# Two local-attention stacks: the unshifted half of the feed forward's input read in place, statistics in two halves, weight loads taken off the shifting steps

## Chip, core and metric

The kernel runs on one core of one Trainium2 chip. The metric is the device time of one execution in microseconds. The median over several executions is compared. Engine names are those of the profile: PE is TensorE (matmuls and transposes), PEld its weight loads, DVE is VectorE, ACT is ScalarE, POOL is GpSimd, and SPq is the queue of the sync engine, which here issues every DMA.

## What is computed

A chain of layers over x of shape (2, 1024, 128), fp32. Two identical stacks of six layers (`local_stack`, tags `l_` and `m_`) take two thirds of the time, and only they are changed. One layer of a stack:

```python
def shift_tokens(t):
    a, s = jnp.split(t, 2, -1)
    s = jnp.pad(s, ((0, 0), (1, 0), (0, 0)))[:, :-1]
    return jnp.concatenate([a, s], -1)
...
def ffn_layer(x, g, bln, W1, b1, W2, b2):
    mu = x.mean(-1, keepdims=True)
    var = ((x - mu) ** 2).mean(-1, keepdims=True)
    xn = (x - mu) / jnp.sqrt(var + 1e-05) * g + bln
    hg = xn @ W1 + b1
    a, gate = jnp.split(hg, 2, -1)
    return a * jax.nn.gelu(gate, approximate=False) @ W2 + b2
for i in range(DEPTH):
    x = attn_layer(shift_tokens(x), Wqkv[i], q_scale[i], k_scale[i], Wo[i]) + x
    x = ffn_layer(shift_tokens(x), ln_g[i], ln_b[i], W1[i], b1[i], W2[i], b2[i]) + x
```

So the feed forward sees each token's own first 64 features and the last 64 of the token before it. `attn_layer` is windowed attention (window 32, 16 heads of 64) with rotary tables.

## The kernel before

**Tiles.** 128 tokens lie on the 128 partitions; a stack has 16 tiles, in 4 groups of 4. `Y` (which is the buffer `XN`) holds the stream, tile by tile. Over six layers there are NL = 96 tiles and FG = 24 groups per stack.

**Steps.** Each engine's program is written out by hand as one loop over steps s. In step s the engines work on several tiles at once: PE projects q and k of tile s+2, takes scores of tile s, v of tile s, and finishes tile s-1 (turn of the weights, `values`, `output_turn`, `output`). `phase(s, k)` gives group g in step 4g+k. A group g of the feed forward goes through: step 4g+4 `shift` (SPq), 4g+5 `statistics` (DVE) and `root` (POOL), 4g+6 `middle` (DVE), `normalise` and `gelu` (ACT), `norm_turn4` and `up` (PE), 4g+7 `down`, 4g+8 the turn for the next layer. Every engine runs its instructions strictly in that written order, with semaphores between engines.

**The shift.** In `shift(g)` the queue waits for `y_add` (DVE has added the attention output of the group's last tile) and then issues copies within the on-chip memory into `xsh`: L1694 the unshifted half of all 128 partitions, L1695 the shifted half of 127 partitions, L1697 partition 127's rows to partition 0, and for even groups L1700, one more row. `statistics(g)` (L1508 to L1516) and `normalise(g)` (L1387) read `xsh`.

**What the queue does besides.** `spread_v(s)` (L1685, L1686, L1688, ten copies a step) waits for `V_out` (ACT's copy of v, L1363) and spreads v into the windows that `values(s)` (PE, L1221) reads one step later. The next layer's weights are loaded by pairs of DMAs (L1655, L1658) in the steps i = 2 to 8 of the 16 of a layer, after the shift where i is 4 or 8, and the feed forward's weights in i = 9.

**ACT around `normalise`.** In a step 4g+6 ACT runs: squares of q, `normalise`, squares of k (L1346), exponents (L1334), `values_out` (L1352, the copy of PE's result O to SBUF), copy of v. PE's `output_turn` (transposes at L1152 with `O` in their name, "the O turn" below) waits for both copies of `values_out`.

**DVE and POOL around it.** After `statistics`, POOL's `root` (L1615) takes the power of the variances, then POOL runs the roots of the next tile (L1574 to L1580) and scales its k (L1586). DVE's `middle` (L1521) is 128x4 elements, and ACT's `normalise` waits for it.

Of the kernel before, what the change touches and what calls it, by code (L numbers as in the profile page):

```python
# [53 lines left out]
def build(nc, t, out):  # L54
    ctx = ExitStack()
    with ctx:
        te, ve, ac, gp, sp = nc.tensor, nc.vector, nc.scalar, nc.gpsimd, nc.sync
        every = []

        def signals(names):  # L60
            made = [ctx.enter_context(nc.semaphore(n)) for n in names.split()]
            every.extend(made)
            return made

        def sb(name, *shape):
            return ctx.enter_context(nc.sbuf_tensor(name, list(shape), F32))
# [3 lines left out]
        V, G = Chain(ve, dve_own), Chain(gp, pool_own)  # L70
# [10 lines left out]
        xn4 = sb("xn4", P, 2, 4, D)  # L81
# [817 lines left out]
        def linear_attention():  # L899
# [170 lines left out]
        rq_out, rk_out, ssr_out, ss_out, rn_out, ms_out, rsum_out, y_add = signals(  # L1070
            "l_rq_out l_rk_out l_ssr_out l_ss_out l_rn_out l_sub_out l_rsum_out l_y_add")
# [4 lines left out]
        v_spread, w_attn, w_rot, w_ffn, shifted = signals("l_v_spread l_w_attn l_w_rot l_w_ffn l_shifted")  # L1076
# [3 lines left out]
        def local_stack(tag):  # L1080
            with ExitStack() as own:
                def sl(name, *shape, dtype=F32):
                    return own.enter_context(nc.sbuf_tensor(tag + name, list(shape), dtype))
                Y = XN
# [22 lines left out]
                mx = sl("mx", P, 2, 8)  # L1107
                sm, rs = sl("sm", P, 2 * 8), sl("rs", P, 2 * 8)
                O, oT = sl("O", P, 8, 2, LD), sl("oT", P, 8, P)
                xsh, xnorm = sl("xsh", P, 2, 4, D), xn4[:, 0, :, :]  # L1110
                xnT = xn4[:, 1, :, :].rearrange("p j d -> p (j d)")
                fst, fmv, frs, fmid, fneg = sl("fst", P, 4, 6), sl("fmv", P, 4, 2), sl("frs", P, 4), sl("fmid", P, 4), sl("fneg", P, 4)
                sums2 = sl("sums2", P, 2 * LH, 2)
                zero, eps = sl("zero", P, 4), sl("eps", P, 4)
                gl, hT = xT4, sl("hT", P, 3, 512)
# [16 lines left out]
                def phase(s, k):  # L1132
                    g, r = divmod(s - k, 4)
                    return g if r == 0 and 0 <= g < FG else None
# [187 lines left out]
                def act():  # L1322
# [60 lines left out]
                    def normalise(g):  # L1383
                        ac.wait_ge(fmid_out, g + 1)
                        at_ge(ac, n_turn, g)
                        for j in range(4):
                            m = ac.activation(xnorm[:, j, :], xsh[:, g % 2, j, :], ACT.Identity, scale=frs[:, j:j + 1], bias=fmid[:, j:j + 1])  # L1387
                        m.then_inc(xnorm_out)

                    def copy_norm(g):  # L1390
# [15 lines left out]
                    for s in range(-2, 4 * FG + 8):  # L1406
# [10 lines left out]
                        if widened is not None:  # L1417
                            normalise(widened)
# [26 lines left out]
                def dve():  # L1445
# [55 lines left out]
                        ve.tensor_tensor(Y[:, i, :], PS[:, 5, 0:D], Y[:, i, :], ALU.add).then_inc(y_add)  # L1501

                    def statistics(g):
                        ve.wait_ge(shifted, 64 * (g // 2 + 1) + 48 * ((g + 1) // 2))
                        V.wait()
                        at_ge(ve, xnorm_out, g)
                        for j in range(4):
                            m = ve.bn_stats(fst[:, j, :], xsh[:, g % 2, j, :])  # L1508
                        V.step(m)
                        V.wait()  # L1510
                        for j in range(4):
                            m = ve.bn_aggr(fmv[:, j, :], fst[:, j, :])
                        V.step(m)
                        V.wait()
                        ve.tensor_tensor(fneg[:, :], zero[:, :], fmv[:, :, 0], ALU.subtract)
                        ve.tensor_tensor(frs[:, :], fmv[:, :, 1], eps[:, :], ALU.add).then_inc(fvar_out)  # L1516
# [51 lines left out]
                def pool():  # L1568
# [63 lines left out]
                    for s in range(-2, 4 * FG + 8):  # L1632
# [15 lines left out]
                        if s % NT == 8 and layer(s) + 1 < DEPTH:  # L1648
                            rotary(layer(s) + 1)

                def transfers():
                    def load_attention(l, k):
                        if k < 12:
                            part = slice(k * 256, (k + 1) * 256)
                            sp.dma_start(wqkv[:, l % 2, part], t["l_wqkv"][l][:, part]).then_inc(w_attn, 16)  # L1655
                        else:
                            half = slice((k - 12) * 4, (k - 11) * 4)
                            sp.dma_start(wo[:, l % 2, half, :], t["l_wo"][l].rearrange("(c p) d -> p c d", p=P)[:, half, :]).then_inc(w_attn, 16)  # L1658
# [31 lines left out]
                    def shift(g):  # L1690
                        par, tiles = g % 2, slice(4 * (g % NG), 4 * (g % NG) + 4)
                        sp.wait_ge(y_add, 4 * g + 4)
                        at_ge(sp, xnorm_out, g)
                        sp.dma_start(xsh[:, par, :, 0:D // 2], Y[:, tiles, 0:D // 2]).then_inc(shifted, 16)  # L1694
                        sp.dma_start(xsh[1:P, par, :, D // 2:], Y[0:P - 1, tiles, D // 2:]).then_inc(shifted, 16)  # L1695
                        inner = slice(tiles.start, tiles.stop - 1)
                        sp.dma_start(xsh[0:1, par, 1:, D // 2:], Y[P - 1:P, inner, D // 2:]).then_inc(shifted, 16)  # L1697
                        if par == 0:
                            last = tiles.stop - 1
                            sp.dma_start(xsh[0:1, 1, 0, D // 2:], Y[P - 1:P, last, D // 2:]).then_inc(shifted, 16)  # L1700

                    load_rotary(0)
                    for k in range(14):
# [2 lines left out]
                    for s in range(-2, 4 * FG + 8):  # L1706
                        if 0 <= s < NL:
                            spread_v(s)
                        done = phase(s, 4)
                        if done is not None:  # L1710
                            shift(done)
                        l, i = layer(s) + 1, s % NT
                        if 0 <= s and l < DEPTH:
                            if i == 1:
                                if l >= 2:
                                    sp.wait_ge(rk_out, NT * (l - 1))
                                load_rotary(l)
                            if i == 2:
                                if l >= 2:
                                    sp.wait_ge(v_pr, NT * (l - 1))  # L1720
                                    sp.wait_ge(out_pr, NT * (l - 1))
                            if 2 <= i < 9:
                                load_attention(l, 2 * (i - 2))
                                load_attention(l, 2 * (i - 2) + 1)
                            if i == 9:
                                if l >= 2:
                                    sp.wait_ge(f_down, NG * (l - 1))
                                load_ffn(l)
# [86 lines left out]
```

## Time and profile before

| | |
|---|---|
| median of 3 runs | 4630.66 us (4624.55 to 4635.63) |
| the profiled execution | 4626.41 us, span 4625.1 us |
| PE busy over the span | 3912.4 us, 85% |
| DVE, ACT, POOL busy | 71%, 55%, 54% |
| the two stacks | from about 1030 to 2735 us and 2905 to 4620 us |
| matmuls and weight loads | 67048 each |

The span is the time from the first to the last instruction. Times below are microseconds from the start of the span. A row of the timeline gives the start, the duration, the engine, the line, the tensors and how many instructions are merged in it; in brackets stands how long the engine sat idle just before, and what released it. Where several merged instructions overlap, the duration is from the first start to the last end.

### The profile page before, as it was taken

Reading aid. Unit: us, or ns where it says so; the run is one execution under the profiler, and the core shown is the slowest. Engines: PE = TensorE matmul, PEld = TensorE weight load, DVE = VectorE, ACT = ScalarE, POOL = GpSimd, SP = SyncE. Lnnn points to the kernel's source line nnn. Section 1 sums busy time; section 2 is a strip of 40 time slices with the busy share of each in tenths; the row PEclk is TensorE's granted clock in tenths of the full one; section 3 lists DMA queues with packets and bytes.
Section 4 is the critical chain, followed back from the end, with each engine's and each line's share of the span. In section 5 each row is a group of like instructions: output and inputs, shape, how many; then the busy total and the mean of one; then the engine's idle time right before and its main releaser. Section 6 shows DMA issues by size and latency. Waiting matters only on the chain. (4 is left out here: it accounts for less than half of the span.)

```text
span 4625.1 us, 159303 instructions
## 1 busy us (share of the span) xinstructions
PE 3912.4 (85%) x67048; PEld 2719.8 (59%) x67048; DVE 3275.4 (71%) x6709; ACT 2524.5 (55%) x4765; POOL 2493.8 (54%) x2057
## 2 busy tenths in 40 slices
PE   6868566628999999999999943699999999999996
PEld 3435344415666666666666632466666666666764
DVE  6749526857777777777777726777777777777773
ACT  2323222205676766667667620466666676676664
POOL 2211001117767667676766700676676767667662
PEclk8869787969999999999999965799999999999998
DMA  0010000003333233333222210232333333233222
GB/s 14 1 32 1 10 1 31 5 18 83 82 83 91 67 90 81 82 87 83 78 73 71 71 29 0 74 91 70 86 80 83 87 83 84 67 92 82 70 68 53
DMA packets 307781, 281.44 MB, mean 61 GB/s; under 512 B 158840, under 2 KB 205568, under 8 KB 307072
## 3 DMA queue, kind: packets, MB, share of 16 engines
q1 hardware_dynamic: 307072, 271.25, 23.0%
q8 instruction: 535, 8.77, 0.8%
q14 instruction: 174, 1.43, 0.1%
HBM read 56.14 MB, written 1.05 MB: 12 GB/s over the span
## 5 line engine op out<-in xcount | busy, mean ns | idle before, releaser
L1346 ACT ACTIVATE l_sq<-PS 128x512 f32<-128x512 f32 x384 | 225.8, 595 | 198.4 <-PE PS L1199 161.1
L1346 ACT ACTIVATE m_sq<-PS 128x512 f32<-128x512 f32 x384 | 225.7, 595 | 198.1 <-PE PS L1199 159.3
L124 POOL TENSOR_TENSOR rstd<-rstd,minus_half 128x4 f32<-128x4 f32 x40 | 41.8, 1044 | 518.7 <-DVE rstd L120 518.7
L1611 POOL TENSOR_TENSOR m_Pm<-m_Pm,m_rs 128x1024 f32<-128x1024 f32 x96 | 182.7, 1903 | 236.2 <-DVE m_rs L1483 236.2
L1611 POOL TENSOR_TENSOR l_Pm<-l_Pm,l_rs 128x1024 f32<-128x1024 f32 x96 | 182.8, 1904 | 235.1 <-DVE l_rs L1483 235.1
L1470 DVE TENSOR_TENSOR m_QR<-PS,m_rot 128x512 f32<-128x512 f32 x192 | 131.8, 687 | 164.8 <-ACT m_sq L1346 164.7
L1470 DVE TENSOR_TENSOR l_QR<-PS,l_rot 128x512 f32<-128x512 f32 x192 | 131.8, 687 | 163.5 <-ACT l_sq L1346 163.5
L1501 DVE TENSOR_TENSOR XN<-PS,XN 128x128 f32<-128x128 f32 x192 | 56.2, 292 | 265.0 <-PE PS L1251 264.9
L1606 POOL TENSOR_TENSOR m_QR<-m_QR,m_UQ 128x1024 f32<-128x1024 f32 x96 | 227.8, 2373 | 24.0 <-DVE m_UQ L1473 24.0
L1606 POOL TENSOR_TENSOR l_QR<-l_QR,l_UQ 128x1024 f32<-128x1024 f32 x96 | 227.7, 2372 | 23.8 <-DVE l_UQ L1473 23.8
L1606 POOL TENSOR_TENSOR m_KR<-m_KR,m_UK 128x1024 f32<-128x1024 f32 x96 | 226.8, 2362 | 0.2 <-DVE m_UK L1473 0.2
L1606 POOL TENSOR_TENSOR l_KR<-l_KR,l_UK 128x1024 f32<-128x1024 f32 x96 | 226.8, 2362 | 0.2 <-DVE l_UK L1473 0.2
L1488 DVE TENSOR_REDUCE l_sums<-l_sq 128x16 f32<-128x1024 f32 x192 | 219.1, 1183 | 0.0
L1488 DVE TENSOR_REDUCE m_sums<-m_sq 128x16 f32<-128x1024 f32 x192 | 219.1, 1183 | 0.0
L1221 PEld LDWEIGHTS PS<-m_V,m_pT 64*32 64x32 f32 x12288 | 132.6, 106 | 120.5 <-issue 66.3
L1221 PEld LDWEIGHTS PS<-l_V,l_pT 64*32 64x32 f32 x12288 | 131.5, 106 | 117.8 <-issue 73.0
L1205 PE MATMUL PS<-m_wqkv,XNT 128*128 128x512 f32 x384 | 194.1, 628 | 0.0
L1205 PE MATMUL PS<-l_wqkv,XNT 128*128 128x512 f32 x384 | 192.5, 624 | 0.0
L1199 PE MATMUL PS<-m_wqkv,XNT 128*128 128x512 f32 x384 | 190.9, 620 | 0.6 <-DVE m_UK L1473 0.6
L1199 PE MATMUL PS<-l_wqkv,XNT 128*128 128x512 f32 x384 | 190.4, 618 | 0.5 <-DVE l_UK L1473 0.5
L1221 PE MATMUL PS<-m_V,m_pT 64*32 64x64 f32 x12288 | 155.1, 228 | 41.6 <-DMA m_V<-m_Vt 27.7
L1251 PE MATMUL PS<-l_wo,l_oT 128*128 128x128 f32 x1536 | 189.1, 277 | 0.7 <-ACT l_oT L1358 0.7
(387 smaller groups left out, 11907.7 us busy)
## 6 DMA issues: line engine op xcount, KB each, us to landing
l_V<-l_Vt SPq DMA_DIRECT2D x576, 128.0 KB
m_V<-m_Vt SPq DMA_DIRECT2D x576, 128.0 KB
l_V<-l_Vt SPq DMA_DIRECT2D x384, 64.0 KB
m_V<-m_Vt SPq DMA_DIRECT2D x384, 64.0 KB
l_wqkv<-l_wqkv_dram SPq DMA_DIRECT2D x72, 128.0 KB, 2.4
m_wqkv<-l_wqkv_dram SPq DMA_DIRECT2D x72, 128.0 KB, 2.4
l_rot<-l_rot_dram SPq DMA_DIRECT2D x24, 256.0 KB, 3.6
m_rot<-l_rot_dram SPq DMA_DIRECT2D x24, 256.0 KB, 3.6
```

The source lines that it names most:

```text
L124: gp.tensor_tensor(rstd[:, g % 2, :], rstd[:, g % 2, :], minus_half[:, 0:4], ALU.pow).then_inc(rstd_out)
L1199: te.matmul(PS[:, 2 + b, :], tile_T(n), weights(n, INNER + b * 512, INNER + (b + 1) * 512), start=True, stop=True).then_inc(k_pr)
L1205: m = te.matmul(PS[:, r, :], tile_T(n), wv, start=True, stop=True)
L1221: m = te.matmul(PS[LW * w:LW * (w + 1), 6 + r, c * LD:(c + 1) * LD], pT[64 * r:64 * r + 64, c, LW * w:LW * (w + 1)], V2[64 * r:64 * r + 64 ...
L1251: m = te.matmul(PS[:, 5, 0:D], oT[:, c, :], wo[:, layer(n) % 2, c, :], start=(c == 0), stop=(c == 7))
L1346: ac.activation(sq[:, c, b * 512:(b + 1) * 512], PS[:, 2 * c + b, :], ACT.Square).then_inc(sq_out)
L1470: ve.tensor_tensor(R[:, n % 2, heads, :], src, over(rot[:, par, 2 * c, i, :], 1, [P, 8, LD]), ALU.mult)
L1488: ve.tensor_reduce(sums2[:, c * LH:(c + 1) * LH, 0], sq[:, c, :].rearrange("p (h d) -> p h d", d=LD), AX, ALU.add).then_inc(ssr_out)
L1501: ve.tensor_tensor(Y[:, i, :], PS[:, 5, 0:D], Y[:, i, :], ALU.add).then_inc(y_add)
L1606: gp.tensor_tensor(R[:, n % 2, :, :], R[:, n % 2, :, :], U[:, :, :], ALU.add).then_inc((aq_out, ak_out)[c])
L1611: gp.tensor_tensor(pm, pm, over(rs[:, :], 2, [P, 16, 2 * LW]), ALU.mult).then_inc(pn_out)
```

## The change

Three edits, in both stacks.

- `xsh` holds only the shifted half (64 features). The copy L1694 is gone, one DMA less per group, 48 in all. `normalise` makes each tile in two ACTIVATEs of 64 columns, one from `Y` and one from `xsh`: eight instead of four per group.
- `statistics` takes `bn_stats` of the first half from `Y` before it waits for the shift, and of the second half from `xsh` behind that wait: eight instructions of 64 columns instead of four of 128. `bn_aggr` joins both.
- The pairs of weight loads go to the steps i = 2, 3, 5, 6, 7, 9, 10 of a layer (`LOADS`), and the feed forward's weights to i = 11, so that no step with a shift (i = 0, 4, 8, 12) issues one.

```diff
-                xsh, xnorm = sl("xsh", P, 2, 4, D), xn4[:, 0, :, :]
+                xsh, xnorm = sl("xsh", P, 2, 4, D // 2), xn4[:, 0, :, :]
...
                         ac.wait_ge(fmid_out, g + 1)
                         at_ge(ac, n_turn, g)
                         for j in range(4):
-                            m = ac.activation(xnorm[:, j, :], xsh[:, g % 2, j, :], ACT.Identity, scale=frs[:, j:j + 1], bias=fmid[:, j:j + 1])
+                            for lo, half in ((0, Y[:, 4 * (g % NG) + j, 0:D // 2]), (D // 2, xsh[:, g % 2, j, :])):
+                                m = ac.activation(xnorm[:, j, lo:lo + D // 2], half, ACT.Identity, scale=frs[:, j:j + 1], bias=fmid[:, j:j + 1])
                         m.then_inc(xnorm_out)
...
                     def statistics(g):
-                        ve.wait_ge(shifted, 64 * (g // 2 + 1) + 48 * ((g + 1) // 2))
-                        V.wait()
+                        ve.wait_ge(y_add, 4 * g + 4)
                         at_ge(ve, xnorm_out, g)
                         for j in range(4):
-                            m = ve.bn_stats(fst[:, j, :], xsh[:, g % 2, j, :])
+                            ve.bn_stats(fst[:, j, 0, :], Y[:, 4 * (g % NG) + j, 0:D // 2])
+                        ve.wait_ge(shifted, 48 * (g // 2 + 1) + 32 * ((g + 1) // 2))
+                        V.wait()
+                        for j in range(4):
+                            m = ve.bn_stats(fst[:, j, 1, :], xsh[:, g % 2, j, :])
                         V.step(m)
...
+                LOADS = (2, 3, 5, 6, 7, 9, 10)
...
-                        sp.dma_start(xsh[:, par, :, 0:D // 2], Y[:, tiles, 0:D // 2]).then_inc(shifted, 16)
-                        sp.dma_start(xsh[1:P, par, :, D // 2:], Y[0:P - 1, tiles, D // 2:]).then_inc(shifted, 16)
+                        sp.dma_start(xsh[1:P, par, :, :], Y[0:P - 1, tiles, D // 2:]).then_inc(shifted, 16)
                         inner = slice(tiles.start, tiles.stop - 1)
-                        sp.dma_start(xsh[0:1, par, 1:, D // 2:], Y[P - 1:P, inner, D // 2:]).then_inc(shifted, 16)
+                        sp.dma_start(xsh[0:1, par, 1:, :], Y[P - 1:P, inner, D // 2:]).then_inc(shifted, 16)
...
-                            if 2 <= i < 9:
-                                load_attention(l, 2 * (i - 2))
-                                load_attention(l, 2 * (i - 2) + 1)
-                            if i == 9:
+                            if i in LOADS:
+                                load_attention(l, 2 * LOADS.index(i))
+                                load_attention(l, 2 * LOADS.index(i) + 1)
+                            if i == 11:
```

The queue SPq of stack `l_`, at the first shift: the copies of v (`l_V<-l_Vt`) of one step, the shift (`l_xsh<-XN`), a load of the next layer's weights, and the copies of v of the next step begin. Before:

```order
L1688 DMA l_V<-l_Vt 64x512 x3
L1694 DMA l_xsh<-XN 128x4x64
L1695 DMA l_xsh<-XN 127x4x64
L1697 DMA l_xsh<-XN 1x3x64
L1700 DMA l_xsh<-XN 1x16x4
L1655 DMA l_wqkv<-l_wqkv_dram 128x256 x2
L1685 DMA l_V<-l_Vt 32x512
```

The same place in the changed kernel (its lines are numbered 5 or 6 higher here):

```order
L1694 DMA l_V<-l_Vt 64x512 x3
L1700 DMA l_xsh<-XN 127x4x64
L1702 DMA l_xsh<-XN 1x3x64
L1705 DMA l_xsh<-XN 1x16x4
L1691 DMA l_V<-l_Vt 32x512
```

The copy of all 128 partitions and the pair of weight loads no longer stand between the two steps' copies of v.

ACT in a step 4g+6, from the squares of q to the copy of O. Before:

```order
L1346 ACTIVATE l_sq<-PS 128x512 x2
L1387 ACTIVATE xn<-l_xsh,l_fmid,l_frs 128x128 x4
L1346 ACTIVATE l_sq<-PS 128x512 x2
L1334 ACTIVATE l_Pm<-l_Pm 128x8x64 x2
L1352 COPY l_O<-PS 128x8x64 x2
```

ACT at the same place in the changed kernel:

```order
L1388 ACTIVATE xn<-XN,l_fmid,l_frs 128x64
L1388 ACTIVATE xn<-l_xsh,l_fmid,l_frs 128x64
L1388 ACTIVATE xn<-XN,l_fmid,l_frs 128x64
L1388 ACTIVATE xn<-l_xsh,l_fmid,l_frs 128x64
L1388 ACTIVATE xn<-XN,l_fmid,l_frs 128x64
L1388 ACTIVATE xn<-l_xsh,l_fmid,l_frs 128x64
L1388 ACTIVATE xn<-XN,l_fmid,l_frs 128x64
L1388 ACTIVATE xn<-l_xsh,l_fmid,l_frs 128x64
L1346 ACTIVATE l_sq<-PS 128x512 x2
L1334 ACTIVATE l_Pm<-l_Pm 128x8x64 x2
L1352 COPY l_O<-PS 128x8x64 x2
```

Four ACTIVATEs became eight half as wide, ahead of the same squares, exponents and copies of O.

DVE at the end of a step 4g+5, from the addition of the attention output to the variances. Before:

```order
L1501 TENSOR_TENSOR XN<-PS,XN 128x128
L1508 BN_STATS l_fst<-l_xsh 128x6 x4
L1512 BN_AGGR l_fmv<-l_fst 128x2 x4
L1515 TENSOR_TENSOR l_fneg<-l_zero,l_fmv 128x4
L1516 TENSOR_TENSOR l_frs<-l_fmv,l_eps 128x4
```

DVE at the same place in the changed kernel:

```order
L1502 TENSOR_TENSOR XN<-PS,XN 128x128
L1508 BN_STATS l_fst<-XN 128x6 x4
L1512 BN_STATS l_fst<-l_xsh 128x6 x4
L1516 BN_AGGR l_fmv<-l_fst 128x2 x4
L1519 TENSOR_TENSOR l_fneg<-l_zero,l_fmv 128x4
L1520 TENSOR_TENSOR l_frs<-l_fmv,l_eps 128x4
```

Four more statistics stand ahead of the variances that POOL waits for. PE's order does not change.

## Rows read from the trace of the kernel before

**Rows 1.** Windows: length, busy PE, PEld, DVE, ACT, POOL (instructions), PEclk, DMA share, GB/s.
```profile
2960.00:4530.00 1570.00, 1523.02 (x30411) 1077.12 (x30412) 1207.08 (x2373) 1081.33 (x2021) 1109.25 (x936) 1.00 0.32 81
```

**Rows 2.** Groups by line: `values` on PE; idle time and its releasers behind the last bar.
```profile
L1221 PE MATMUL PS<-m_V,m_pT 64*32 64x64 f32 x12288 | 155.1, 228 | 41.6 <-DMA m_V<-m_Vt 27.7 <-issue 12.7 <-ACT m_pT L1340 0.5
```

**Rows 3.** Timeline, ACT and PE, in two groups of the feed forward.
```profile
3798.34 1.65 ACT L1387 ACTIVATE xn<-m_xsh,m_fmid,m_frs 128x128 f32<-128x128 f32 x4 [2.88 <-DVE m_fmid L1521]
3801.89 1.05 ACT L1352 COPY m_O<-PS 128x512 f32<-128x512 f32 x2
3802.99 1.09 PE L1152 MATMUL PS<-ident,m_O 128*128 128x128 f32 x8 [0.42 <-ACT m_O L1352]
...
4477.05 1.65 ACT L1387 ACTIVATE xn<-m_xsh,m_fmid,m_frs 128x128 f32<-128x128 f32 x4 [2.88 <-DVE m_fmid L1521]
4481.70 1.09 PE L1152 MATMUL PS<-ident,m_O 128*128 128x128 f32 x8 [0.74 <-ACT m_O L1352]
```

**Rows 4.** Groups by line, ACT: the same kind of ACTIVATE at two widths.
```profile
L1387 ACT ACTIVATE xn<-m_xsh,m_fmid,m_frs 128x128 f32<-128x128 f32 x96 | 39.5, 482 | 83.9 <-DVE m_fmid L1521 83.9
L1395 ACT ACTIVATE xn<-PS,m_lnb,m_lng 128x512 f32<-128x512 f32 x24 | 19.4, 810 | 1.2 <-PE PS L1152 1.2
```

**Rows 5.** Timeline, DVE and POOL, statistics of one group to its `middle`.
```profile
3792.48 0.86 DVE L1508 BATCH_NORM_STATS2 m_fst<-m_xsh 128x6 f32<-128x128 f32 x4
3794.10 1.02 POOL L1615 TENSOR_TENSOR m_frs<-m_frs,minus_half 128x4 f32<-128x4 f32 x1 [0.24 <-DVE m_frs L1516]
3796.38 1.90 POOL L1586 TENSOR_TENSOR m_KR<-m_KR,m_rn 128x1024 f32<-128x1024 f32 x1
3797.32 0.98 DVE L1521 TENSOR_TENSOR m_fmid<-m_fneg,m_frs 128x4 f32<-128x4 f32 x1
```

**Rows 6.** Timeline of SPq from one step's shift to the next step's copies of v.
```profile
3026.38 0.66 SPq L1694 DMA_DIRECT2D m_xsh<-XN  x1
...
3027.90 6.56 SPq L1697 DMA_DIRECT2D m_xsh<-XN  x1
3034.50 0.56 SPq L1700 DMA_DIRECT2D m_xsh<-XN  x1
3035.11 1.05 SPq L1655 DMA_DIRECT2D m_wqkv<-l_wqkv_dram  x2
3036.26 0.57 SPq L1685 DMA_DIRECT2D m_V<-m_Vt  x1
```

**Rows 7.** Timeline: ACT's copy of v in that step, then PE behind the late copies.
```profile
3033.10 1.01 ACT L1363 COPY m_Vt<-PS 128x1024 f32<-128x1024 f32 x1 [0.84 <-PE PS L1205]
3043.57 1.65 ACT L1387 ACTIVATE xn<-m_xsh,m_fmid,m_frs 128x128 f32<-128x128 f32 x4 [2.88 <-DVE m_fmid L1521]
3046.49 2.06 PE L1221 MATMUL PS<-m_V,m_pT 64*32 64x64 f32 x128 [2.56 <-DMA m_V<-m_Vt]
3050.83 1.04 PE L1152 MATMUL PS<-ident,m_O 128*128 128x128 f32 x8
```

**Rows 8.** Timeline of PE at four other idle gaps of about 2 us, and at a usual one.
```profile
2250.23 1.81 PE L1221 MATMUL PS<-l_V,l_pT 64*32 64x64 f32 x128 [2.04 <-DMA l_V<-l_Vt]
2251.97 3.12 PE L1205 MATMUL PS<-l_wqkv,XNT 128*128 128x512 f32 x4
...
3321.99 1.81 PE L1221 MATMUL PS<-m_V,m_pT 64*32 64x64 f32 x128 [2.19 <-DMA m_V<-m_Vt]
...
1077.18 1.06 PE L1152 MATMUL PS<-ident,l_KR 128*128 128x128 f32 x8 [2.16 <-DVE l_UK L1473]
...
2682.06 0.34 PE L1221 MATMUL PS<-l_V,l_pT 64*32 64x64 f32 x15 [2.06 <-issue]
2682.33 1.99 PE L1205 MATMUL PS<-l_wqkv,XNT 128*128 128x512 f32 x4
...
3868.04 1.48 PE L1221 MATMUL PS<-m_V,m_pT 64*32 64x64 f32 x128 [0.83 <-DMA m_V<-m_Vt]
```

**Rows 9.** Windows: the granted clock (PEclk) behind the gap at 3321.99.
```profile
3323.00:3326.00 3.00, 3.00 (x60) 1.73 (x43) 2.96 (x6) 1.07 (x2) 0.76 (x2) 0.50 0.00 0
```

More of the change, by code:

```diff
@@ L1109, in local_stack @@
                 O, oT = sl("O", P, 8, 2, LD), sl("oT", P, 8, P)
-                xsh, xnorm = sl("xsh", P, 2, 4, D), xn4[:, 0, :, :]
+                xsh, xnorm = sl("xsh", P, 2, 4, D // 2), xn4[:, 0, :, :]
                 xnT = xn4[:, 1, :, :].rearrange("p j d -> p (j d)")
-                fst, fmv, frs, fmid, fneg = sl("fst", P, 4, 6), sl("fmv", P, 4, 2), sl("frs", P, 4), sl("fmid", P, 4), sl("fneg", P, 4)
+                fst, fmv, frs, fmid, fneg = sl("fst", P, 4, 2, 6), sl("fmv", P, 4, 2), sl("frs", P, 4), sl("fmid", P, 4), sl("fneg", P, 4)
                 sums2 = sl("sums2", P, 2 * LH, 2)
@@ L1511, in statistics @@
                         for j in range(4):
-                            m = ve.bn_aggr(fmv[:, j, :], fst[:, j, :])
+                            m = ve.bn_aggr(fmv[:, j, :], fst[:, j, :, :])
                         V.step(m)
@@ L1693, in shift @@
                         at_ge(sp, xnorm_out, g)
-                        sp.dma_start(xsh[:, par, :, 0:D // 2], Y[:, tiles, 0:D // 2]).then_inc(shifted, 16)
-                        sp.dma_start(xsh[1:P, par, :, D // 2:], Y[0:P - 1, tiles, D // 2:]).then_inc(shifted, 16)
+                        sp.dma_start(xsh[1:P, par, :, :], Y[0:P - 1, tiles, D // 2:]).then_inc(shifted, 16)
                         inner = slice(tiles.start, tiles.stop - 1)
-                        sp.dma_start(xsh[0:1, par, 1:, D // 2:], Y[P - 1:P, inner, D // 2:]).then_inc(shifted, 16)
+                        sp.dma_start(xsh[0:1, par, 1:, :], Y[P - 1:P, inner, D // 2:]).then_inc(shifted, 16)
                         if par == 0:
                             last = tiles.stop - 1
-                            sp.dma_start(xsh[0:1, 1, 0, D // 2:], Y[P - 1:P, last, D // 2:]).then_inc(shifted, 16)
+                            sp.dma_start(xsh[0:1, 1, 0, :], Y[P - 1:P, last, D // 2:]).then_inc(shifted, 16)
                     load_rotary(0)
```

## Prediction

> **What bounds the kernel now.** I read the windows first. In the steady part of a stack PE is busy for 1523 of 1570 us at a full granted clock, while DVE, ACT and POOL stand between 69% and 77% [rows 1]. So PE sets the time, and an edit counts only where it moves a wait of PE. Next come the groups by line, for PE's waits. The largest is ahead of `values`: 27.7 us in the second stack on the copies of v that SPq issues [rows 2]. This is what the change aims at. Last the timeline, at the step in which both the shift's aftermath and `normalise` lie. There the second wait shows: the O turn waits for ACT's copy of O, 0.42 us in one group and 0.74 us in another [rows 3].
>
> This second wait is rigid. From the start of the four ACTIVATEs of `normalise` to the end of the second copy of O, ACT runs without a gap: 3801.89 + 1.05 - 3798.34 = 4.60 us, and PE starts the O turn 4.65 us after `normalise` began; at 4477.05 and 4481.70 it is 4.65 again [rows 3]. I read this distance for all 46 groups whose `normalise` lies beside attention steps (23 per stack). In 41 of them ACT's stretch is 4.60 to 4.69 us. In the other five the copies of v came so late that they set the O turn, as at 3043.57 to 3050.83, 7.26 us, behind a PE wait of 2.56 us [rows 7]. So ACT is the least busy engine of the stretch, and yet it has no slack exactly where the change adds to it.
>
> **The queue.** Removed from every shift: L1694, 0.66 us and 0.04 to the next issue. Removed from two of four shifts in the layers that load: a pair of weight loads, 1.05 us and 0.1 [rows 6]. The copies of v could have begun when ACT's copy ended, at 3034.11, and began at 3036.26, 2.15 us late [rows 6, 7]. The change makes them 0.7 us earlier, or 1.85 us with the loads. The moved pairs and the 13 DMAs of `load_ffn` now stand in steps without a shift, behind that step's copies of v. Those steps last 15 to 20 us, the ten copies take 6.3 to 7.7 us of them by my reading, and `load_ffn` some 6 us, so they cost nothing; in a 15 us step with a late start their cover would be gone and the next copies of v would slip by a microsecond.
>
> **ACT.** The same ACTIVATE takes 482 ns at 128 columns and 810 ns at 512, 0.85 ns a column, so 427 ns at 64 [rows 4]. The four take 1.65 us together [rows 3], a start every (1.65 - 0.48) / 3 = 0.39 us. At 64 columns that is 0.335 us, and eight take 7 x 0.335 + 0.43 = 2.77 us: **+1.12 us per group**. Bounds: 0 if a half cost half, which the 0.85 ns a column exclude; 1.56 if each kept its 0.39 us. I take the fit.
>
> **DVE.** Four statistics of 128 columns take 0.86 us [rows 5], about 0.2 us each. Eight halves take between 0.86 us (each costs half) and 1.65 us (each costs as much as a whole): 0 to +0.8 us, nothing less. No row has a 64-column one. I take **+0.3 us**, a little under the middle, since an instruction of 128 columns is not all overhead. The wait for the shift between the halves is long met in the steady part, where DVE never idles ahead of L1508. This delay does reach ACT: POOL's `root` waits 0.24 us for DVE's variances, POOL then scales k until 3796.38 + 1.90 = 3798.28, and DVE's tiny L1521, started at 3797.32, ends with it at 3798.30 after 0.98 us [rows 5]; 0.04 us later `normalise` starts. I read this as DVE waiting for POOL, so the 0.3 us pass on to ACT through POOL. If L1521 were merely slow they would not, and the sum would be 41 x 0.3 = 12 us smaller. The Trainium skill, SBUF — State Buffer, "Who interferes with whom", says that a VectorE instruction with two SBUF inputs and a GpSimd instruction that reads SBUF shut each other out for a whole instruction; by that rule the first reading holds, and the trace's equal ends agree.
>
> **PE.** The new O turn starts 0.3 + 1.12 + 4.65 = 6.07 us after the old start of `normalise`, unless the copies of v come later still. Taken against the old start in each group, 41 groups lose 0.7 to 1.42 us, 1.36 on average (less than 1.42 where v was last by a little): +55.6 us. The five groups gain: the one at 3043.57 has 7.26 - 6.07 = 1.2 us [rows 7], all five 7.6 us. Behind the O turn PE runs its transposes, the output, six `up` pairs and the next step without another wait on ACT, so nothing gives the time back. At the stacks' ends the queue's 0.7 us earlier and ACT's 1.12 us later leave 0.3 us over. Together **+48 us**.
>
> **The clock.** The gap of PE ahead of the O turn grows to 1.9 us from 0.42 and to 2.2 us from 0.74; where a wait of about 0.8 us at `values` goes, that time joins it. By the same working 37 of the 46 gaps become 2.0 to 2.6 us. The trace of before has five gaps of PE of this size in the steady part. Behind 2.04, 2.19 and 2.56 us PE ran slow: `values` took 1.81 to 2.06 us instead of 1.48, and v's matmuls 3.12 instead of 1.99 [rows 7, 8]; the granted clock there was 0.50, that is 1.2 GHz [rows 9]. Behind 2.06 and 2.16 us it did not fall [rows 8], nor behind any shorter gap. One fall costs 0.33 + 1.13 = 1.46 us where both rows stand [rows 8]; part of another may meet an idle PE, so I take 1.3. Three in five of 37 gaps give 22 falls, **+29 us**; with none 0, with all 48.
>
> **Sum.** 48 + 29 = 77 us. The profiled execution took 4626.4 us (span 4625.1), 4.3 us under the median of the runs; on the median it gives 4708 us.
>
> **Rivals.**
>
> 1. *The gaps grow but the clock holds.* For it: two gaps of this size without a fall, one of them ahead of transposes as here (1077.18) [rows 8]. Against it: the three others. 4631 + 48 = 4679 us.
>
> 2. *Faster: the queue sets the step, and ACT's growth is hidden.* The place is the O turn. If ACT could overlap the halves, or if the O turn were not on ACT's end, only the queue's relief would remain: each wait at `values` falls by 0.7 or 1.85 us, or to nothing, 25 us over the 46 groups, against 27.7 us that the second stack shows in all [rows 2]. It gives 4606 us. It decides only if ACT and DVE together grow by less than about 0.3 us a group, as 41 x 0.3 = 12 us is then less than what the queue gives. The rigid 4.60 us speak against it.
>
> 3. *The queue gains more than I count.* L1697, a copy of three rows, holds SPq for 6.56 us, and L1700, one row too, for 0.56 [rows 6]. So L1697 pays for what was issued ahead of it. If that is both big copies, dropping one halves it and v is never late: the five groups gain another 3 us and each stack's end 3 us, -9 us on whichever sum. The Trainium skill, DMA: Bandwidth & Descriptors, "Why a DMA increments its semaphore by 16 and not by 1", has a 127-partition copy on a single DMA engine and a 128-partition one on 16. By it the 127-partition copy alone makes the stall, and it stays at its 6.5 us; the trace before has no shift without L1694 to tell.
>
> 4. *No change within 0.2%:* growth and relief cancel. That needs a growth of about 0.2 us a group, outside the bounds of ACT.
>
> **Chances.** Growth with clock falls 0.60 (4690 to 4738 us); growth, hardly a fall 0.27 (4664 to 4690); no change 0.05; faster 0.08. Rival 3 shifts either of the first two and has 0.2 of its own within them. The range 4664 to 4738 us takes in the first two with ACT's growth from 0.9 to 1.56 us and 0 to 35 falls. About 0.2% (9 us) is what a measurement of this kernel can tell from no change; slower 0.87, same 0.05, faster 0.08.
>
> **What the new profile would show.** The four ACTIVATEs become eight in 2.7 to 2.8 us, and from their start to the end of the copy of O 5.7 us. PE's wait ahead of the O turn, put down to ACT, grows from a few microseconds in all to some 80, and the wait for v's copies at `values` falls below half. POOL's `root` waits about 0.3 us longer. The granted clock of the stacks' steady stretches drops from 1.00 to 0.97 or 0.98. L1697 keeps its 6.5 us. The prediction would be wrong if the eight took no more than 2 us, if the copy of O were not what the O turn waits for, or, in size, if nearly no gap or every gap brought the clock down.

## The result, and the profile after

| | before | changed |
|---|---|---|
| median | 4629.9 us (4624.55 to 4635.63, 4 runs) | 4680.61 us (4677.5 to 4696.67, 4 runs) |
| profiled execution | 4626.41 us, span 4625.1 us | 4677.5 us, span 4676.2 us |

The changed kernel takes 1.0117 times as long, 95% interval 1.0101 to 1.0132: 50.7 us slower by the medians. The forecast was 4708 us with a range of 4664 to 4738, so the sign and the range held and the point was 27 us too high. The case that came true is not the one that the prediction held likeliest (growth with clock falls, 4690 to 4738 us, chance 0.60) but its rival 1, growth while the clock hardly falls (4664 to 4690 us, chance 0.27).

The groups by line show where the time went: PE, with the idle time behind the last bar. Before, beside the row of `values` in [rows 2]:

```profile
L1221 PE MATMUL PS<-l_V,l_pT 64*32 64x64 f32 x12288 | 154.9, 226 | 38.1 <-DMA l_V<-l_Vt 22.0 <-issue 14.8
L1152 PE MATMUL PS<-ident,m_O 128*128 128x128 f32 x768 | 101.4, 276 | 6.0 <-ACT m_O L1352 5.8
L1152 PE MATMUL PS<-ident,l_O 128*128 128x128 f32 x768 | 101.3, 275 | 9.0 <-ACT l_O L1352 8.8
```

Changed:

```profile
L1221 PE MATMUL PS<-l_V,l_pT 64*32 64x64 f32 x12288 | 155.0, 226 | 21.6 <-DMA l_V<-l_Vt 10.2 <-issue 10.0
L1221 PE MATMUL PS<-m_V,m_pT 64*32 64x64 f32 x12288 | 154.4, 226 | 27.8 <-DMA m_V<-m_Vt 15.5 <-issue 11.0
L1152 PE MATMUL PS<-ident,l_O 128*128 128x128 f32 x768 | 103.5, 279 | 46.2 <-ACT l_O L1352 46.2
L1152 PE MATMUL PS<-ident,m_O 128*128 128x128 f32 x768 | 102.6, 277 | 40.9 <-ACT m_O L1352 40.9
```

The wait ahead of `values` in the second stack fell from 41.6 us [rows 2] to 27.8; over both stacks from 79.7 to 49.4. That is what the change aimed at, 30.3 us. But the wait ahead of the O turn, which was 9.0 and 6.0 us, is now 46.2 and 40.9: 72.1 us more. The balance of the two is +41.8 us. These are sums of one execution each; in a second profile of the changed kernel (`after_again` below) they are 57.5 us at `values` and 83.0 at the O turn, so either can be off by several us.

The timeline of one group of the feed forward (3766.42 and on), and of another in which PE's clock fell (3701.68 and on):

```profile
3766.42 0.44 ACT L1388 ACTIVATE xn<-XN,m_fmid,m_frs 128x64 f32<-128x64 f32 x1 [3.16 <-DVE m_fmid L1525]
3766.76 0.43 ACT L1388 ACTIVATE xn<-m_xsh,m_fmid,m_frs 128x64 f32<-128x64 f32 x1
...
3768.75 0.42 ACT L1388 ACTIVATE xn<-m_xsh,m_fmid,m_frs 128x64 f32<-128x64 f32 x1
3771.08 1.05 ACT L1352 COPY m_O<-PS 128x512 f32<-128x512 f32 x2
...
3772.18 1.09 PE L1152 MATMUL PS<-ident,m_O 128*128 128x128 f32 x8 [2.39 <-ACT m_O L1352]
3773.11 0.60 PE L1152 MATMUL PS<-ident,xn 128*128 128x128 f32 x4
3773.54 1.04 PE L1152 MATMUL PS<-ident,m_KR 128*128 128x128 f32 x8
3774.42 1.04 PE L1152 MATMUL PS<-ident,m_QR 128*128 128x128 f32 x8
...
3701.68 1.77 PE L1152 MATMUL PS<-ident,m_O 128*128 128x128 f32 x8 [2.04 <-ACT m_O L1352]
3703.24 1.06 PE L1152 MATMUL PS<-ident,xn 128*128 128x128 f32 x4
3704.09 1.65 PE L1152 MATMUL PS<-ident,m_KR 128*128 128x128 f32 x8
3705.58 1.04 PE L1152 MATMUL PS<-ident,m_QR 128*128 128x128 f32 x8
```

From the start of `normalise` to the end of the copy of O it is 3771.08 + 1.05 - 3766.42 = 5.71 us, against 4.60 before [rows 3]; the O turn starts at +5.76. This distance is 5.70 or 5.71 in 44 of the 46 groups. The gap ahead of the O turn is 2.39 us here, 1.84 on average over the 46 groups. In the second group the same transposes ran slower: from the O turn to the turn of q it is 3705.58 - 3701.68 = 3.90 us instead of 3774.42 - 3772.18 = 2.24, so this fall of the clock cost 1.66 us. The windows give the granted clock there, in the column after POOL's:

```profile
3701.60:3705.00 3.40, 3.32 (x17) 3.33 (x18) 3.37 (x5) 2.76 (x5) 1.61 (x1) 0.55 0.16 39
...
1075.00:2640.00 1565.00, 1495.83 (x29716) 1058.73 (x29716) 1191.98 (x2414) 1085.13 (x2070) 1082.11 (x914) 0.99 0.30 78
2980.00:4570.00 1590.00, 1520.61 (x30338) 1074.13 (x30337) 1217.75 (x2459) 1101.56 (x2101) 1105.79 (x929) 1.00 0.30 77
```

0.55 is a stretch almost all at 1.2 GHz; over the stacks' steady parts the mean stays at 0.99 and 1.00. I counted a fall where the transposes in the 5 us behind an O turn last over 12% longer than usual. There are 8 of them in the 46 groups, all behind gaps of 1.90 to 2.47 us. From the start of the O turn to the start of `output` it is 3.11 us without a fall; behind the eight it is 1.62 to 1.67 us more, 13 us together. Against them stand the three falls of before behind waits at `values` [rows 7, 8]: in the changed kernel no such wait in the steady part of a stack is longer than 1.63 us, and none has a fall behind it. At the prediction's 1.46 us each that takes back 4. 41.8 + 13 - 4 = 51 us, and the spans differ by 51.1.

The two halves of the work, by line:

```profile
L1388 ACT ACTIVATE xn<-XN,m_fmid,m_frs 128x64 f32<-128x64 f32 x96 | 41.2, 429 | 88.6 <-DVE m_fmid L1525 88.6
L1388 ACT ACTIVATE xn<-m_xsh,m_fmid,m_frs 128x64 f32<-128x64 f32 x96 | 40.8, 425 | 0.0
L1508 DVE BATCH_NORM_STATS2 m_fst<-XN 128x6 f32<-128x64 f32 x96 | 14.4, 212 | 0.3
L1512 DVE BATCH_NORM_STATS2 m_fst<-m_xsh 128x6 f32<-128x64 f32 x96 | 14.1, 208 | 8.8 <-DMA m_xsh<-XN 8.8
```

An ACTIVATE of half the width takes 425 to 429 ns instead of 482 [rows 4]. The Trainium skill, ScalarE: Activation LUTs, "What ACT_TABLE_LOAD costs", has 186 ns, 0.833 ns a column and about 93 ns for each pointer operand (here the scale and the bias); worked out for 64 columns that is an estimate of 425 ns, and the trace agrees. The statistics take 28.5 us per stack instead of 20.6 (24 times the 0.86 us of [rows 5]): 0.33 us a group more.

Last, the queue at a shift, and DVE and POOL around `middle`:

```profile
3053.88 0.77 SPq L1700 DMA_DIRECT2D m_xsh<-XN  x1
3054.69 6.52 SPq L1702 DMA_DIRECT2D m_xsh<-XN  x1
3061.26 0.54 SPq L1705 DMA_DIRECT2D m_xsh<-XN  x1
3061.90 0.57 SPq L1691 DMA_DIRECT2D m_V<-m_Vt  x1
```

```profile
3762.18 1.02 POOL L1619 TENSOR_TENSOR m_frs<-m_frs,minus_half 128x4 f32<-128x4 f32 x1 [0.82 <-DVE m_frs L1520]
3764.46 1.90 POOL L1590 TENSOR_TENSOR m_KR<-m_KR,m_rn 128x1024 f32<-128x1024 f32 x1
...
3765.12 1.26 DVE L1525 TENSOR_TENSOR m_fmid<-m_fneg,m_frs 128x4 f32<-128x4 f32 x1
```

The copies of v now follow the shift at once, but the copy of three rows (L1702) still holds the queue for 6.52 us, although only one copy stands ahead of it. And `middle`, 512 products, ends at 3766.38 together with POOL's scaling of k at 3766.36, after 1.26 us; `normalise` starts 0.04 us later.

### The profile page after: what moved, and what is told of

It is laid out like the page before. It is cut to its first block and busy times, and to the rows that moved or that the text cites. A ratio compares the mean times of both kernels' runs of the same rounds, so it can differ in the third digit from the quotient of the medians.

```text
span 4676.2 us, 159685 instructions
## 1 busy us (share of the span) xinstructions
PE 3924.4 (84%) x67048; PEld 2732.7 (58%) x67048; DVE 3301.9 (71%) x6901; ACT 2577.9 (55%) x4957; POOL 2492.9 (53%) x2057
## 3 DMA queue, kind: packets, MB, share of 16 engines
HBM read 56.14 MB, written 1.05 MB: 12 GB/s over the span
## 5 line engine op out<-in xcount | busy, mean ns | idle before, releaser
L124 POOL TENSOR_TENSOR rstd<-rstd,minus_half 128x4 f32<-128x4 f32 x40 | 41.8, 1045 | 520.0 <-DVE rstd L120 520.0
L1251 PE MATMUL PS<-m_wo,m_oT 128*128 128x128 f32 x1536 | 189.1, 277 | 0.7 <-ACT m_oT L1358 0.7
```

The lines of the kernel that those rows point to most:

```text
L1251: m = te.matmul(PS[:, 5, 0:D], oT[:, c, :], wo[:, layer(n) % 2, c, :], start=(c == 0), stop=(c == 7))
```

## Experiments

**1 to 3: each part alone.** Each is the kernel before with one part of the change.

`loads_only`: the weight loads moved, nothing else.

```diff
+                LOADS = (2, 3, 5, 6, 7, 9, 10)
...
-                            if 2 <= i < 9:
+                            if i in LOADS:
...
-                            if i == 9:
+                            if i == 11:
```

> The kernel before with the weight loads taken off the shifting steps and nothing else. Theory (ACT's chain of normalise, squares, exponents and copy of O sets the O turn): the queue is 1.15 us earlier in 20 of the 48 groups, but the O turn sits on ACT's chain in most of them, so only the groups with a wait of about 2 us at values gain; -3 to -9 us against before. Rival (the late copies of v set the step): up to 1.15 us in each of the 20, -15 to -23 us.

Measured: 4621.12 us (12 runs), 0.9984 times before (0.9975 to 0.9993), that is 8 us faster. In the groups by line, PE:

```profile
L1221 PE MATMUL PS<-m_V,m_pT 64*32 64x64 f32 x12288 | 154.8, 226 | 31.5 <-DMA m_V<-m_Vt 16.9 <-issue 13.5
...
L1152 PE MATMUL PS<-ident,m_O 128*128 128x128 f32 x768 | 101.5, 276 | 13.8 <-ACT m_O L1352 13.8
```

The wait at `values` falls by 10.1 us in this stack, and the wait at the O turn rises by 7.8, from 6.0 to 13.8. Over both stacks it is 12.0 less and 10.2 more. The two waits are in series: most of what PE no longer waits at `values` it waits half a step later for ACT.

`stats_halves`: the statistics in eight instructions of 64 columns, both halves from the full `xsh`, behind the wait.

```diff
...
-                            m = ve.bn_stats(fst[:, j, :], xsh[:, g % 2, j, :])
+                            ve.bn_stats(fst[:, j, 0, :], xsh[:, g % 2, j, 0:D // 2])
+                        for j in range(4):
+                            m = ve.bn_stats(fst[:, j, 1, :], xsh[:, g % 2, j, D // 2:])
...
-                            m = ve.bn_aggr(fmv[:, j, :], fst[:, j, :])
+                            m = ve.bn_aggr(fmv[:, j, :], fst[:, j, :, :])
```

> The kernel before with eight bn_stats of 64 columns in place of four of 128, both halves still from the full copy and behind the wait. Theory (the delay passes from DVE over POOL's root and scaling of k to DVE's middle and ACT's normalise): 0.28 us in some 41 groups, +8 to +13 us; ACT's idle time ahead of normalise goes from 2.88 to 3.16 us. Rival (DVE has slack there, the idle time grew for another reason): within 3 us of before.

Measured: 4638.85 us (11 runs), 1.0019 times before (1.0011 to 1.0028), 9.8 us slower. The idle time of ACT ahead of `normalise` grew from 83.9 us [rows 4] to 89.4:

```profile
L1387 ACT ACTIVATE xn<-m_xsh,m_fmid,m_frs 128x128 f32<-128x128 f32 x96 | 39.6, 482 | 89.4 <-DVE m_fmid L1523 89.4
```

That is 0.23 us a group of the 0.33 that the statistics grew. The view of the line of `middle` (shortest, median and longest in ns) shows where it passes:

```profile
L1523 DVE TENSOR_TENSOR m_fmid<-m_fneg,m_frs x24: 163/1268/1333, 3052.3 to 4615.4; 128x4 f32<-128x4 f32 x24
```

Before, the median was 978 ns. The product itself grew by 0.29 us, and ACT's growth is no more than that, so `middle` passes the delay of POOL on, as the prediction read it, and does not absorb it.

`norm_halves`: the eight ACTIVATEs alone, both halves from the full `xsh`.

```diff
-                            m = ac.activation(xnorm[:, j, :], xsh[:, g % 2, j, :], ACT.Identity, scale=frs[:, j:j + 1], bias=fmid[:, j:j + 1])
+                            for lo in (0, D // 2):
+                                m = ac.activation(xnorm[:, j, lo:lo + D // 2], xsh[:, g % 2, j, lo:lo + D // 2], ACT.Identity, scale=frs[:, j:j + 1], bias=fmid[:, j:j + 1])
```

> The kernel before with normalise in eight ACTIVATEs of 64 columns in place of four of 128, all from the full copy; queue and statistics as before. Theory: +1.11 us in some 41 groups, +38 to +48 us, and PE's wait ahead of the O turn rises from 15 us to some 60. Rival (the loss of the change comes from reading the stream's buffer beside DVE and the queue, or from the shorter copy): under +10 us.

Measured: 4682.76 us (4 runs), 1.0111 times before (1.0093 to 1.013), 53.7 us slower, 6 us above the expected range.

```profile
L1221 PE MATMUL PS<-m_V,m_pT 64*32 64x64 f32 x12288 | 155.3, 227 | 41.1 <-DMA m_V<-m_Vt 24.6 <-issue 15.7
...
L1152 PE MATMUL PS<-ident,m_O 128*128 128x128 f32 x768 | 102.9, 278 | 28.7 <-ACT m_O L1352 28.7
```

The wait at the O turn is 56.0 us over both stacks, 41 more than before, the wait at `values` 2.9 more, and 3 falls behind the O turn add 5 us; some 5 us of the 53.7 stay unexplained. The parts add up: -8 + 9.8 + 53.7 = +55.5, and the smaller copy, which has no run alone, is left with about -5 of the measured +50.7, no more than the intervals of the three runs leave open. The eight ACTIVATEs are the cause of the slowdown.

**4: more of the suspected cost.** `twelve` is the changed kernel with four more ACTIVATEs of 64 columns in each `normalise`, into a buffer that nothing reads.

```diff
+                xtra = sl("xtra", P, 4, D // 2)
...
+                        for j in range(4):
+                            m = ac.activation(xtra[:, j, :], xsh[:, g % 2, j, :], ACT.Identity, scale=frs[:, j:j + 1], bias=fmid[:, j:j + 1])
```

> The changed kernel with four more ACTIVATEs of 64 columns behind the eight, written to a buffer that nothing reads, so that the gap of PE ahead of the O turn grows by 4 x 0.34 = 1.35 us, from about 2 to about 3.3 us. Theory (ACT's chain): +59 us on the changed kernel from the chain alone, 4740 us. Clock: if a gap of about 2 us lies just at the edge, most of the gaps of 3.3 us bring the clock down, some 35 falls of 1.3 us more, 4785 us; if the fall depends little on the gap's length, no more than 10 falls, 4745 us.

Measured: 4799.52 us (4 runs), 1.0364 times before (1.0347 to 1.0382), 119 us over the changed kernel. Groups by line, and one O turn of the timeline:

```profile
L1153 PE MATMUL PS<-ident,m_O 128*128 128x128 f32 x768 | 113.1, 296 | 74.4 <-ACT m_O L1353 74.4
...
3858.18 1.73 PE L1153 MATMUL PS<-ident,m_O 128*128 128x128 f32 x8 [3.73 <-ACT m_O L1353]
```

The waits at the O turn come to 146.7 us, 59.6 more, 1.3 us a group as four starts of 0.33 us make it. The clock fell behind 38 of the 46. The rest of the 119 us is mostly the clock: from the O turn to `output` the falls cost 69 us here, since six of them cost over 2.5 us each, against 13 in the changed kernel, and 59.6 + 56 leaves 3 over. Of the two cases expected it is the one with falls behind most gaps, 15 us above its 4785.

**5 and 6: the wait itself taken away.** In `mid_pool`, which is the changed kernel otherwise, POOL makes the product that `middle` made, right behind its own `root`; DVE has no `middle`. `before_mid_pool` is the same edit on the kernel before.

```diff
...
-                            middle(widened)
...
-                        gp.tensor_tensor(frs[:, :], frs[:, :], minus_half[:, 0:4], ALU.pow).then_inc(froot_out)
+                        G.step(gp.tensor_tensor(frs[:, :], frs[:, :], minus_half[:, 0:4], ALU.pow))
+                        G.wait()
+                        gp.tensor_tensor(fmid[:, :], fneg[:, :], frs[:, :], ALU.mult).then_inc(fmid_out)
```

> The changed kernel with the 128x4 product of middle made by POOL right behind its root instead of by DVE a step later, so that normalise can start about 2.5 us earlier, in ACT's idle time of 3.16 us. Theory: ACT's chain no longer ends after PE's v matmuls, the 87 us of PE's wait ahead of the O turn fall under 15, and some of it comes back as waits at values: 4600 to 4615 us, faster than both kernels. Rival (the eight ACTIVATEs cost as much wherever they stand, or POOL's 0.3 us more delays k and q): no more than 20 us under the changed kernel.

> The kernel before with the product of middle on POOL in the same way. Theory: PE's 15 us ahead of the O turn go, and the waits for the copies of v, 50 us there, now set the O turn in every group with one: 4612 to 4622 us. The difference to the changed kernel with the same move is what the queue's relief is worth once ACT is out of the way, 5 to 20 us. Rival (the move gains nothing by itself): 4626 to 4634 us.

Measured: `mid_pool` 4587.08 us (4 runs), 0.9906 times before (0.9892 to 0.9919); `before_mid_pool` 4622.84 us (11 runs), 0.9982 (0.9973 to 0.9991), 0.8 us above the expected range. On the changed kernel the edit takes away 94 us, on the kernel before 7. `mid_pool`'s timeline, POOL, ACT and PE, and its groups by line:

```profile
3697.99 1.02 POOL L1612 TENSOR_TENSOR m_frs<-m_frs,minus_half 128x4 f32<-128x4 f32 x1 [0.85 <-DVE m_frs L1520]
3699.09 0.20 POOL L1614 TENSOR_TENSOR m_fmid<-m_fneg,m_frs 128x4 f32<-128x4 f32 x1
...
3699.33 0.44 ACT L1388 ACTIVATE xn<-XN,m_fmid,m_frs 128x64 f32<-128x64 f32 x1 [0.26 <-POOL m_fmid L1614]
...
3703.99 1.05 ACT L1352 COPY m_O<-PS 128x512 f32<-128x512 f32 x2
...
3705.45 1.04 PE L1152 MATMUL PS<-ident,m_O 128*128 128x128 f32 x8
```

```profile
L1221 PE MATMUL PS<-m_V,m_pT 64*32 64x64 f32 x12288 | 153.8, 226 | 23.3 <-issue 11.5 <-DMA m_V<-m_Vt 11.0
...
L1152 PE MATMUL PS<-ident,m_O 128*128 128x128 f32 x768 | 100.7, 274 | 1.2 <-ACT m_O L1352 1.2
```

`normalise` now starts 0.32 us after the end of the root, where it was 3766.42 - 3763.20 = 3.22 us. These 2.9 us are more than the whole gap ahead of the O turn: that wait goes from 87.1 to 2.4 us over both stacks, the clock falls behind none of the 46 turns, and the eight ACTIVATEs cost PE nothing. 84.7 us of wait and 13 us of clock are 98, against 94 measured; I had expected more of it to come back as a wait at `values`, which stayed (50.9 us against 49.4). In the kernel before, the O turn had only 15 us of wait to give: 12.6 of them went, and 6.7 came back at `values` (86.4 us against 79.7). The two kernels with the edit lie 36 us apart, where 5 to 20 were expected, and the wait at `values` accounts for it (86.4 against 50.9): with ACT out of the way the queue's relief counts.

Of the 2.9 us only a part is the product's own time. DVE started it at 3765.12, 1.92 us after POOL's root had ended, since rotary products of q stand ahead of it in DVE's program, and then took 1.26 us; on POOL it takes 0.20. An earlier place in DVE's own program was not tried.

**7 and 8: the queue's stall.** `split` is the changed kernel with the shifted copy in two pieces; `mid_pool_split` the same on `mid_pool`.

```diff
...
-                        sp.dma_start(xsh[1:P, par, :, :], Y[0:P - 1, tiles, D // 2:]).then_inc(shifted, 16)
+                        sp.dma_start(xsh[1:113, par, :, :], Y[0:112, tiles, D // 2:]).then_inc(shifted, 16)
+                        sp.dma_start(xsh[113:P, par, :, :], Y[112:P - 1, tiles, D // 2:]).then_inc(shifted, 16)
```

> The changed kernel with the shifted copy of 127 partitions cut into one of 112 and one of 15 partitions, one DMA more. Theory on the stall: the 127-partition copy runs on one DMA engine and the copy of three rows behind it waits for it; cut, the 6.5 us of the three-row copy fall under 1.5 us. Theory on the time: the O turn stays on ACT's chain, so only the last groups and the ends of the two stacks gain, where DVE waits 8.8 us for the shift: -10 to -20 us on the changed kernel. Rival (the stall is of the three-row copy itself, or of the number of rows): it keeps 6.5 us and the time is the changed kernel's.

> The changed kernel with both: the product on POOL and the shifted copy cut in 112 and 15 partitions. Theory: with ACT out of the way and the queue never late, the gains add and a little more, as waits at values behind a shift go too: 4575 to 4595 us. Rival (once ACT's chain is shorter something else, DVE or POOL, holds the O turn): not under 4600 us.

Measured: `split` 4694.65 us (4 runs), 1.0134 times before (1.012 to 1.0148); `mid_pool_split` 4580.23 us (4 runs), 0.9887 (0.9871 to 0.9904), faster than both kernels of the change. The queue of `split`:

```profile
3063.97 0.67 SPq L1700 DMA_DIRECT2D m_xsh<-XN  x1
3064.69 1.40 SPq L1701 DMA_DIRECT2D m_xsh<-XN  x1
3066.13 0.76 SPq L1703 DMA_DIRECT2D m_xsh<-XN  x1
3066.94 0.59 SPq L1706 DMA_DIRECT2D m_xsh<-XN  x1
```

The stall is gone: the copy of three rows issues in 0.76 us instead of 6.52, so it was the copy of 127 partitions that it paid for. The Trainium skill, DMA: Bandwidth & Descriptors, "Why a DMA increments its semaphore by 16 and not by 1", spreads a transfer over the largest number of engines up to 16 that divides the partition count, which is 1 for 127, 16 for 112 and 15 for 15; the trace agrees as far as it shows, in that the stall goes when this copy is cut. The expected gain of `split`, 10 to 20 us, does not show in its time, which is 14 us longer. The part of it at the stacks' ends did come: there PE waits for `normalise` itself, ahead of the transposes of `xn`, and this wait fell from 30.5 us over both stacks to 18.6. But its wait ahead of the O turn was 92.1 us against 87.1, since that turn still stands 5.76 us behind `normalise`, the wait at `values` was 54.7 against 49.4, and its clock fell 18 times instead of 8. Whether these falls belong to the kernel the next two runs ask.

**9 and 10: the same two kernels again.**

> The changed kernel once more, beside the version with the shifted copy in two pieces. In the first profiles PE's waits ahead of the O turn were 87 us here and 92 us there, but the clock fell behind 8 of these waits here and behind 18 there, about 1.8 us each. Theory A, the number of falls belongs to the kernel (its exact gaps decide): the two differ again by 10 to 18 us, and again some 8 falls against some 18. Theory B, the falls are scattered by chance from run to run and the four runs of the first comparison happened to lie apart: the difference shrinks below 7 us, with the counts of falls overlapping. I lean to A, since three of four runs of the split version lay above three of four of the changed kernel: 4681 us here.

> The shifted copy in pieces of 112 and 15 partitions, once more. Theory A: 4690 to 4698 us and 15 to 20 falls, 10 to 18 us over the changed kernel of the same comparison. Theory B: 4680 to 4690 us and anything from 5 to 15 falls.

Measured, in one comparison: `after_again` 4686.52 us (4 runs, 4683.0 to 4689.14; 1.0117 times before, 1.0103 to 1.0131), `split_again` 4689.66 us (5 runs, 4674.41 to 4696.44; 1.0117, 1.0099 to 1.0135). So theory B: the difference of 14 us is down to 3, and the one profiled execution of `split_again` had 10 falls and a span of 4673.1 us, where that of `split` had 18 and 4693.2. Its wait ahead of `xn` is 18.6 us again, against 30.5 in `after_again`; what takes these 12 us back in the medians, the profiles do not show for certain. The gaps ahead of the 46 O turns in the profiles, in classes, with the falls behind them:

| gap, us | changed | again | split | again | norm_halves | twelve |
|---|---|---|---|---|---|---|
| under 0.6 | 2, 0 falls | 2, 0 | 2, 0 | 2, 0 | 12, 0 | 2, 0 |
| 0.6 to 1.9 | 17, 0 | 20, 0 | 15, 0 | 15, 0 | 28, 0 | 1, 0 |
| 1.9 to 2.6 | 27, 8 | 24, 10 | 29, 18 | 29, 10 | 6, 3 | 2, 1 |
| over 2.6 | 0 | 0 | 0 | 0 | 0 | 41, 37 |

Behind gaps of the same size the clock falls at one place and not at another: in the first four profiles together behind 46 of 109 gaps of 1.9 to 2.6 us.

**11 and 12: is half a copy worth having?** `whole_mid_loads` is the kernel before with the moved loads and the product on POOL: the whole input copied, four statistics, four ACTIVATEs. `whole_mid_loads_split` also cuts its 127-partition copy.

```diff
...
                         sp.dma_start(xsh[:, par, :, 0:D // 2], Y[:, tiles, 0:D // 2]).then_inc(shifted, 16)
-                        sp.dma_start(xsh[1:P, par, :, D // 2:], Y[0:P - 1, tiles, D // 2:]).then_inc(shifted, 16)
+                        sp.dma_start(xsh[1:113, par, :, D // 2:], Y[0:112, tiles, D // 2:]).then_inc(shifted, 16)
+                        sp.dma_start(xsh[113:P, par, :, D // 2:], Y[112:P - 1, tiles, D // 2:]).then_inc(shifted, 16)
```

> The kernel before with the moved loads and with the product of the mean and the root on POOL, but the whole input copied, four statistics and four ACTIVATEs: against the change with that product on POOL (4587 us) it differs by the halves alone. Theory A: once the O turn waits for ACT no longer, the eight ACTIVATEs cost nothing and the 0.7 us less on the queue count in full at the wait for the copies of v, so copying one half is worth 5 to 25 us: 4592 to 4612 us here. Theory B: the halves still cost ACT time somewhere, and the whole copy is as good or better: 4575 to 4587 us.

> The same with the shifted half in pieces of 112 and 15 partitions, so that no issue on SPq holds the queue for 6.5 us. Theory A (what is issued ahead of the copies of v is all that counts): 1.6 us more room than with the stall even with the 128-partition copy in place, so the wait for v is as small as in the best version so far and the time comes to 4577 to 4588 us. Theory B (the stall was hidden in most steps, as the gain of 7 us in the best version suggests): 5 to 10 us under the version without the split, 4590 to 4605 us.

Measured: 4604.57 us (5 runs), 0.994 times before (0.9926 to 0.9953), and 4580.3 us (5 runs), 0.9891 (0.9877 to 0.9906). PE at `values` and ahead of `xn`, in `whole_mid_loads` and then in `whole_mid_loads_split`:

```profile
L1221 PE MATMUL PS<-l_V,l_pT 64*32 64x64 f32 x12288 | 157.5, 226 | 31.7 <-DMA l_V<-l_Vt 15.8 <-issue 13.7 <-ACT l_pT L1340 0.5
L1152 PE MATMUL PS<-ident,xn 128*128 128x128 f32 x192 | 29.8, 279 | 30.3 <-ACT xn L1387 30.3
```

```profile
L1221 PE MATMUL PS<-l_V,l_pT 64*32 64x64 f32 x12288 | 158.8, 225 | 26.2 <-issue 15.9 <-DMA l_V<-l_Vt 9.1
L1152 PE MATMUL PS<-ident,xn 128*128 128x128 f32 x192 | 29.8, 279 | 18.4 <-ACT xn L1387 18.4
```

Both in theory A's ranges. With the stall in place, copying one half is worth 0.9940 - 0.9906 of the time, 16 us, and the wait at `values` shows 13 of them (64.3 us against 50.9 over both stacks, though two profiles of one kernel differ by 8 there). Without the stall the whole copy (0.9891) and the half (0.9887) are equal. Cutting the copy is worth 24 us here: 11.6 at `values` and 11.9 ahead of `xn` at the stacks' ends. And the moved weight loads, which alone gave 8 us, give 18 behind the product on POOL (`before_mid_pool` 4622.84, `whole_mid_loads` 4604.57). The saving that the change was built on came out of a stall that cutting one copy removes.

## Why the prediction came out as it did

- **What bounds the kernel.** Right: PE, with two waits of its own, and the second of them rigid.
- **ACT, +1.12 us per group.** Right: 5.71 - 4.60 = 1.11, from the straight line through 128 and 512 columns. `norm_halves` puts 54 us on it alone.
- **DVE, +0.3 us, passed on through POOL.** Right: 0.33 us of statistics, ACT's idle time ahead of `normalise` from 2.88 to 3.16, and `stats_halves` gives 10 us of the forecast 12. One sign was put wrongly: POOL's `root` does not wait longer in the changed kernel, where its waits sum to 85.4 us over both stacks against 86.5 before; it runs later.
- **The queue.** Right in kind: the wait at `values` for the copies of v fell from 22.0 + 27.7 to 10.2 + 15.5 us, a little over half, where below half was forecast. L1697's successor keeps its 6.5 us, so rival 3 is out, and `split` shows that the 127-partition copy makes them. The moved loads cost nothing that counts, since alone they make the kernel faster. Their relief, though, came back mostly at the O turn (12.0 us less at `values`, 10.2 more there).
- **PE, +48 us.** Nearly right: 41.8 us by the two waits.
- **The clock, +29 us.** This step failed, in size: "Three in five of 37 gaps give 22 falls". The gaps of 2.0 us and over were 23, not 37, out of 46 whose mean was 1.84 us; and the share, three in five from five gaps of before, was 46 of 109 over four profiles, 8 of 27 in the profiled execution. The price of a fall, 1.3 us, was 1.66. It came to 8 falls and 13 us, 16 us less than forecast. The sum also put at nothing the three falls of before that went with the waits at `values`, about 4 us. The granted clock stayed at 0.99 and 1.00 instead of 0.97 or 0.98. Three in five did occur in one profile, that of `split`: one execution's count is a draw, and the four of the changed kernel spread over 19 us.

So the 26 us between 77 and 51 are 16 of falls behind the O turn, 6 of the two waits, and about 4 of the falls of before that went. That rival 1's 4679 us meets the measured 4680.61 so closely is in part luck: it has 6 us too much of waits and no falls, where the falls cost 9 on balance. Expectations behind the prediction failed too. For `split` the relief at the stacks' ends came but does not show in the time; for `mid_pool` I reckoned with a wait at `values` that did not come; and for the pair of kernels with the product on POOL I put the queue's relief at 20 us or less, where it was 36.

## What to carry to other kernels

A wait removed is worth something only as far as the next wait in series does not rise: the moved loads alone took 12.0 us from `values` and gave 10.2 to the O turn, and were worth 18 us instead of 8 once the O turn no longer waited. And work added where an engine has no slack counts in full, however idle the engine is on average: eight short ACTIVATEs in such a stretch of ACT brought 72 us at the O turn against 30 saved at `values`. Before splitting instructions to save a transfer, look for what sits just ahead of that stretch: making 512 products on POOL, a step earlier, gave 94 us, and cutting a copy of 127 partitions in two made the transfer saving itself unnecessary. A term that rests on a clock fall needs more than five gaps of evidence, and a comparison that hangs on it more than one profile.

## What the hardware showed unexpectedly

- The product of 128x4 elements took a median of 1.26 us on DVE in the changed kernel (0.98 before) and 0.20 us on POOL. It ends with POOL's scaling of k in both kernels, and where it meets no such work it takes 0.16 us. The view of its line:

```profile
L1525 DVE TENSOR_TENSOR m_fmid<-m_fneg,m_frs x24: 161/1264/1502, 3069.8 to 4651.4; 128x4 f32<-128x4 f32 x24
```

- A copy of 127 partitions costs its own issue 0.77 us and the next DMA on the queue 6.5. Cut into 112 and 15 they take 0.67, 0.96 and, for the next, 0.75 (medians; the second is 1.40 in the rows above).
- Ahead of the O turn, in the six profiles of the table, PE's clock fell behind 50 of 117 idle gaps of 1.9 to 2.6 us, 37 of 41 longer ones and none of 96 of 0.6 to 1.9 us; two executions of one kernel differ by 8 falls and 20 us. What decides between falling and not behind equal gaps, no run here tells.
